# A fused transformer layer: the second MLP projection through its rank-64 factors, its residual added on GpSimd, deeper input buffers

## The reference

```python
h = hidden_states + attn_out
x2 = _layernorm(h, ln2_g, ln2_b)
hmid = jax.nn.gelu(x2 @ fc1_U @ fc1_V + fc1_b, approximate=True)   # 512 wide
mlp_out = hmid @ fc2_U @ fc2_V + fc2_b     # fc2_U: 512 x 64, fc2_V: 64 x 128
return h + mlp_out
# outside: x + (that) + experts(xn)
```

## Time and profile before

| What | Value |
|---|---|
| median of 3 runs | 1167.45 us (1165.19 to 1182.71) |
| profiled execution, its own time | 1171.44 us |
| its span | 1169.7 us |
| mean granted TensorE clock | 0.91 |
| TensorE matmul busy | 1035.9 us (89%) |
| VectorE busy | 721.8 us (62%) |
| ScalarE busy | 562.6 us (48%) |
| GpSimd busy | 387.7 us (33%) |

### The profile page before, as it was taken

How to read it: one execution, slowest core, us unless ns; L and a number is a source line. 1 busy time by engine, 2 the same in 40 slices (tenths; PEclk the granted TensorE clock), 3 DMA queues, 4 the chain that set the end, 5 groups by cost and what they waited for, 6 DMA issues and landing times. The chain is left out here.

```text
span 1169.7 us, 29046 instructions
## 1 busy us (share of the span) xinstructions
PE 1035.9 (89%) x7812; PEld 813.7 (70%) x7813; DVE 721.8 (62%) x3239; ACT 562.6 (48%) x1285; POOL 387.7 (33%) x509
## 2 busy tenths in 40 slices
PE   0697388999999999999999996999999999949997
PEld 0596165665656656566666664999999999948987
DVE  6255575776767677567577783445444444446887
ACT  0372134555546545355355565555555555525442
POOL 1003633333334324233234431444444444430110
PEclk9655668999989999799799998999999999979999
DMA  7569533443434434344243411122121122144774
GB/s 223 172 217 358 119 72 73 105 117 92 112 82 100 108 96 107 63 100 107 73 112 83 102 56 44 56 64 58 55 67 57 56 58 61 49 150 128 227 226 149
DMA packets 146698, 127.35 MB, mean 109 GB/s; under 512 B 18560, under 2 KB 128512, under 8 KB 146624
## 3 DMA queue, kind: packets, MB, share of 16 engines
q1 hardware_dynamic: 117344, 72.45, 22.7%
q0 software_dynamic: 17808, 47.35, 15.2%
q10 hardware_dynamic: 11472, 6.75, 2.2%
HBM read 57.68 MB, written 43.13 MB: 86 GB/s over the span
## 5 line engine op out<-in xcount | busy, mean ns | idle before, releaser
L1201 DVE CUSTOM_DVE_ANT_0 att_masked_st<-att_m_ps,att_mask_st 128x128 bf16<-128x128 f32 (+1 forms) x1024 | 312.8, 354 | 142.0 <-PE att_m_ps L916 63.5
L1106 ACT ACTIVATE att_probs<-att_t_ps 128x512 f32<-128x512 f32 x384 | 228.0, 597 | 228.2 <-PE att_t_ps L940 217.2
L834 POOL DMA_INDIRECT slot_x<-att_xs,att_slot_now x128 | 128.0, 1000 | 307.3 <-PE att_t_ps L940 285.5
L1377 POOL DMA_INDIRECT y_scratch<-moe_y,moe_row_now x136 | 131.0, 963 | 171.4 <-DVE moe_y L1519 113.5
L1513 DVE TENSOR_TENSOR moe_hidden<-moe_gate,moe_up_ps 128x352 f32<-128x352 f32 x136 | 70.8, 521 | 122.9 <-issue 67.9
L940 PE MATMUL att_t_ps<-att_mask_ts,att_ident_b 128*128 128x256 bf16 (+1 forms) x384 | 127.5, 332 | 0.0
L1436 PE MATMUL moe_y_ps<-w_down,moe_hidden_t 128*128 (+1 forms) x816 | 113.7, 275 | 1.8 <-issue 1.2
L1473 ACT ACTIVATE moe_gate<-moe_gate_ps 128x352 f32<-128x352 f32 x136 | 63.1, 464 | 100.3 <-PE moe_up_ps L1419 100.3
L1436 PEld LDWEIGHTS moe_y_ps<-w_down,moe_hidden_t 128*128 128x128 f32 (+1 forms) x816 | 101.7, 191 | 2.5 <-issue 2.4
L939 PE MATMUL att_t_ps<-att_odd_stack,att_k_stack 97*128 97x512 f32 x192 | 86.7, 452 | 1.9 <-DMA att_odd_stack<-att_neg_max 1.6
L955 PE MATMUL att_pv_ps<-att_probs,att_v_ones 128*32 128x256 f32 x1024 | 86.5, 411 | 0.0
(11 more groups left out here) (248 smaller groups left out, 2151.3 us busy)
## 6 DMA issues: line engine op xcount, KB each, us to landing
slot_x<-prep_blank POOLq DMA_DIRECT2D x17, 516.0 KB, 12.7
moe_x<-slot_x SPq DMA_DIRECT2D x34, 258.0 KB, 3.0
att_xs<-xn_scratch SPq DMA_DIRECT2D x32, 256.0 KB
att_k_stack<-att_k_hi POOLq DMA_DIRECT2D x64, 128.0 KB
mlp_rows<-y_scratch POOLq DMA_DIRECT2D x16, 512.0 KB, 4.8
xn_scratch<-prep_xn SPq DMA_DIRECT2D x16, 256.0 KB, 2.4
xt_scratch<-prep_xt SPq DMA_DIRECT2D x16, 256.0 KB, 2.1
att_xt<-xt_scratch SPq DMA_DIRECT2D x16, 256.0 KB, 2.6
```

Source lines behind the costliest of these rows:

```text
L834: pool.indirect_dma_start(env["slot_x"][:], bass.IndirectOffsetOnAxis(ap=slot_now[c.parity][:, col:col + 1], axis=0), xs[c.parity][:, t, k ...
L1106: act.activation(probs[:, m % PT, :], t_ps[m % 2][:], ACT.Exp).then_inc(exp_done, 1)
L1201: last = dve.tensor_tensor_reduce(out=masked_st[m % 2][:, part], in0=m_ps[m % 2][:, part], in1=mask_st[:, SEQ - width:], scale=1.0, scalar ...
L1377: pool.indirect_dma_start(env["y_dram"][:], bass.IndirectOffsetOnAxis(ap=row_now[q.parity][:, t:t + 1], axis=0), y[c.parity][:], None).the ...
```

## The change

1. `prepare` no longer forms `w2`. The two factors are loaded as they are: `fc2_left` (512 x 64 as 4 pieces of 128 x 64) and `fc2_right`, which holds `fc2_V` twice, in partitions 0 to 63 and 64 to 127 (one more DMA). Eight TensorE instructions and two ScalarE copies go.
2. fc2 of a chunk becomes `fc2_rank` (four fp32 matmuls with a 128 x 64 piece of `fc2_left` as weights and 512 columns of `mid` moving; pieces 0 and 2 add up in partitions 0 to 63 of the bank `r_ps`, pieces 1 and 3 in partitions 64 to 127), a copy of `r_ps` to SBUF by ScalarE, and `fc2_out` one step later (four fp32 matmuls, 128 x 128 weights from the copy, 128 columns of `fc2_right`) into a single bank `o_ps`. The contraction over 128 partitions in `fc2_out` adds the two halves.
3. x + h + bias is formed in place in the x buffer by two POOL instructions a chunk (`add_ahead`), behind POOL's load of the expert rows of the same chunk. VectorE keeps L1775 and L1780, one step later than before. At the start POOL issues its four loads ahead of `w1_lo`.
4. h is read once. h and x have four buffers; h of the first four chunks is loaded without a wait, later ones six chunks ahead of the store.

```diff
-                def fc2(c, t):
-                    if t == 0:
-                        pe.wait_ge(mid_ready, HCH * (c.index + 1))
-                        if not (isinstance(c.index, int) and c.index < 2):
-                            pe.wait_ge(total_ready, c.index - 1)
-                    for k in range(HCH):
-                        last = pe.matmul(o_ps[c.parity][:, t * P:(t + 1) * P], mid[c.parity][:, k, t * P:(t + 1) * P], w2[:, k, :],
-                                         start=(k == 0), stop=(k == HCH - 1))
+                def fc2_rank(c, pair):
+                    pe.wait_ge(mid_ready, HCH * c.index + 2 * pair + 2)
+                    if pair == 0 and not (isinstance(c.index, int) and c.index == 0):
+                        pe.wait_ge(rank_ready, c.index)
+                    for j in range(2):
+                        last = pe.matmul(r_ps[j * RANK_MLP:(j + 1) * RANK_MLP, :], fc2_left[:, 2 * pair + j, :], mid[c.parity][:, 2 * pair + j, :],
+                                         start=(pair == 0), stop=(pair == 1), skip_group_check=True)
+                    if pair == 1:
+                        last.then_inc(rank_done, 1)
+                def fc2_out(c):
+                    pe.wait_ge(rank_ready, c.index + 1)
+                    if not (isinstance(c.index, int) and c.index == 0):
+                        pe.wait_ge(fc2_taken, c.index)
+                    for t in range(TPC):
+                        last = pe.matmul(o_ps[:, t * P:(t + 1) * P], rank[:, t * P:(t + 1) * P], fc2_right[:], start=True, stop=True)
+                    last.then_inc(fc2_done, 1)
...
-                    for k in range(HCH):
-                        if left > 1:
-                            fc1(at(half, d + 1), k)
-                        fc2(at(half, d), k)
+                    if left > 1:
+                        fc1(at(half, d + 1), 0)
+                    if not first:
+                        fc2_out(at(half, d - 1))
+                    if left > 1:
+                        fc1(at(half, d + 1), 1)
+                    fc2_rank(c, 0)
+                    if left > 1:
+                        fc1(at(half, d + 1), 2)
+                        fc1(at(half, d + 1), 3)
+                    fc2_rank(c, 1)
...
+                def copy_rank(c):
+                    act.wait_ge(rank_done, c.index + 1)
+                    if not (isinstance(c.index, int) and c.index == 0):
+                        act.wait_ge(fc2_done, c.index)
+                    act.copy(rank[:], r_ps[:]).then_inc(rank_ready, 1)
...
+                def add_ahead(quad, k):
+                    index = AHEAD * quad + k
+                    pool.wait_ge(h_loaded[k], 16 * (quad + 1))
+                    pool.wait_ge(x_loaded[k], 16 * (quad + 1))
+                    pool.tensor_tensor(x[k][:], x[k][:], h[k][:], ALU.add).then_inc(h_added, 1)
+                    pool.wait_ge(h_added, index + 1)
+                    pool.tensor_tensor(x[k][:], x[k][:], fc2_bias[:].unsqueeze(1).to_broadcast([P, TPC, P]), ALU.add).then_inc(x_ready, 1)
...
-                    dve.tensor_tensor(sums[:], x[c.parity][:], h_again[c.parity][:], ALU.add).then_inc(sum_step, 1)
-                    dve.tensor_tensor(sums[:], sums[:], fc2_bias[:].unsqueeze(1).to_broadcast([P, TPC, P]), ALU.add).then_inc(sum_step, 1)
-                    dve.tensor_tensor(sums[:], o_ps[c.parity][:].rearrange("p (t d) -> p t d", d=P), sums[:], ALU.add).then_inc(sum_step, 1)
+                    dve.tensor_tensor(sums[:], o_ps[:].rearrange("p (t d) -> p t d", d=P), x[k][:], ALU.add).then_inc(fc2_taken, 1)
...
-                    add_up(quad, d)
+                    add_up(quad, d - 1)
```

More of the change, by code:

```diff
@@ L323, in _ @@
                 load(fc1_v[:], w["fc1_V"])
-                load(fc2_u[:], w["fc2_U"].rearrange("(c p) r -> p c r", p=P))
-                load(fc2_v[:], w["fc2_V"])
+                load(fc2_left[:], w["fc2_U"].rearrange("(c p) r -> p c r", p=P))
+                for k in range(2):
+                    load(fc2_right[k * RANK_MLP:(k + 1) * RANK_MLP, :], w["fc2_V"])
                 act.dma_start(w_router[:], w["Wr"]).then_inc(router_loaded, 16)
@@ L1556, in mlp_and_combine @@
         mid = s.two("mid", [P, HCH, CHUNK])
-        h = s.two("h", [P, TPC, P])
-        x = s.two("x", [P, TPC, P])
-        h_again = s.two("h_again", [P, TPC, P])
+        rank = s.sb("rank", [P, CHUNK])
         total = s.two("total", [P, TPC, P])
         AHEAD = 4
+        h = [s.sb(f"h{k}", [P, TPC, P]) for k in range(AHEAD)]
+        x = [s.sb(f"x{k}", [P, TPC, P]) for k in range(AHEAD)]
         rows = [s.sb(f"rows{k}", [P, 2 * TPC, P]) for k in range(AHEAD)]
         t_ps = [s.ps(f"t_ps{k}", [P, CHUNK]) for k in range(2)]
+        r_ps, o_ps = s.ps("r_ps", [P, CHUNK]), s.ps("o_ps", [P, CHUNK])
         f_ps = [s.ps(f"f_ps{k}", [P, CHUNK]) for k in range(HCH)]
-        o_ps = [s.ps(f"o_ps{k}", [P, CHUNK]) for k in range(2)]
         ln_step = s.sem("ln_step")
@@ new lines, in load_x @@
+                def load_x(index):
+                    k = index % AHEAD
+                    if index >= AHEAD:
+                        sp.wait_ge(fc2_taken, index - (AHEAD - 1))
+                    sp.dma_start(x[k][:], env["x_tiles"][:, ds(index * TPC, TPC), :]).then_inc(x_loaded[k], 16)
+                for k in range(AHEAD):
+                    load_h(k)
+                    load_x(k)
+                for k in range(2):
+                    load_h(AHEAD + k)
+                for c in range(chunks):
+                    if c + AHEAD < chunks:
+                        load_x(c + AHEAD)
+                    sp.wait_ge(total_ready, c + 1)
+                    sp.dma_start(env["out_tiles"][:, ds(c * TPC, TPC), :], total[c % 2][:]).then_inc(stored[c % 2], 16)
+                    if c + AHEAD + 2 < chunks:
+                        load_h(c + AHEAD + 2)
@@ L1671, in step @@
+                def fc2_out(c):
[5 more added lines that the diff above has]
+                    last.then_inc(fc2_done, 1)
                 def step(half, d, left):
+                    c = at(half, d)
+                    first = isinstance(c.index, int) and c.index == 0
@@ L1690, in _ @@
                 step(chunks // 2 - 1, 1, 1)
+                fc2_out(at(chunks // 2 - 1, 1))
             @block.scalar
@@ L1718, in _ @@
                     gelu(at(0, 0), k, True)
-                step(0, 0, 3, True)
+                step(0, 0, 3)
                 step(0, 1, 3)
@@ L1724, in _ @@
                 step(chunks // 2 - 1, 0, 2)
+                step(chunks // 2 - 1, 1, 1)
+                copy_rank(at(chunks // 2 - 1, 1))
             @block.vector
```

150 lines of the change are left out of this document (61 added, 89 removed).

## The result

The changed kernel takes 1180.58 us (median of 20 runs), the kernel before, run beside it, 1170.74 us (median of 20 runs). The ratio is 1.0071 with a 95% interval of 1.0042 to 1.01: slower by 0.7%, where a gain of 0.95% was forecast, and above the forecast's own range of 1153 to 1161 us as well as the wider one of 1150 to 1171. The profiled execution has a span of 1175.6 us, 5.9 above the profiled one before; 1158.6 had been predicted.

A forecast was written before the change was run, and what follows sets the result against it. Took TensorE and VectorE both as full in the last stage. TensorE's step falls from 6.89 to 6.26 us; with start, tail and fold, 11.1 us less: 1167.45 - 11 = 1156.5 us, own range 1153 to 1161.

The forecast's parts named there:

- the wider one: Whole-kernel range of 1150 to 1171 us, taking in rival 3, most of rival 2 and the three-round form.
- What POOL's adds cost: Last stage: POOL's two adds, 2.6 us a chunk, hold only VectorE's weighted sums, by 0 to 1.3 us, 0.6 taken.
- signs of being wrong: Last stage: rank records evenly spaced at 0.43 us, VectorE's step over 7 us, or TensorE waiting for `copy_rank`.
- The second rival: Last stage: POOL's adds hold VectorE fully, 2.6 us, VectorE's step 8.2 us, total 1171 us; chance 0.15.
- The start: Start of the last stage: 1.0 us charged for POOL holds, bounds 0 to 2.6; fc1 of chunk 1 at 1055.8.
- are not waited for at once: Start of the last stage: extra h, x and expert-row loads issued ahead make nothing wait at once.
- rival 1: Last stage, `fc2_rank`: pairs do not run together, 3.46 instead of 1.73 us, total 1184 us; chance 0.13 with three-round form.
- three-round form: Last stage, `fc2_rank`: records start in program order, +0.43 us twice a chunk, 1170 us; chance 0.13 with rival 1.
- Rival 3: TensorE in the last stage: mode changes cost nothing where other waits cover them, 6.7 us less, 1150 us; chance 0.10.
- The fold's 0.35 us: Fold in `prepare`: dropping four transposes saves about 0.86 us, one more DMA costs about 0.5; net -0.35 us.
- B: Experiments' theory, last stage: TensorE's new chain (rank matmuls, copy, `fc2_out`) has its own wait that sets the 8.0 us step.
- C: Experiments' theory, last stage: the deeper loads come late or delay others; step near 8.0 us.

The follow-up runs named there:

- e7: Kernel before, with two idle POOL adds on buffers of their own behind the loads of the last 12 chunks; one run, 1193.85 us.
- e1: Changed kernel with the two adds a chunk moved from POOL to VectorE; ratio to before 0.9913 (0.9833 to 0.9993).
- e9: Changed kernel with SP loading h of chunks 0 to 3 before x, and POOL making `w1_lo` before its four loads; one run, 1173.8 us.
- e6: Changed kernel with adds on VectorE, normalise on ScalarE and a chunk's rank matmuls all in one row; one run, 1153.29 us.
- e2: Changed kernel with one POOL add a chunk instead of two, leaving out the fc2 bias; ratio to before 1.0053 (0.9994 to 1.0113).
- e3b: Changed kernel with POOL's adds of a chunk waiting for the next chunk's normalise; one run, 1168.74 us; the same kernel timed again, ratio 1.0001.
- e5: Changed kernel with the normalise moved to ScalarE as four activations, the adds staying on POOL; one run, 1181.92 us.

## Why the prediction was wrong

**The step that failed** is "What POOL's adds cost". It found that POOL can hold VectorE, with the 0.91 us of the earlier trace rows, and then took only the instructions that read two SBUF tensors for holdable. The normalise reads one tensor and two columns of scalars; I counted it, by name, among the cover under which the first add would lie free. e7 shows the reverse: it is held for the whole length of each add. So the hold was 2.7 us a chunk in place of 0 to 1.3 (0.6 taken), VectorE's step 8.17 us on average in place of 5.54 to 6.84, and the 14 steps 103.8 us in place of 86.3. These 17.5 us, 2.5 of the start and 0.9 of the tail, less the 4.2 by which the stages ahead were shorter (0.3 of it forecast, for the fold), are the 17 us between the forecast span and the measured one. Of the prediction's signs of being wrong, a VectorE step over 7 us is the one that came.

The second rival had the mechanism ("or a normalise that is held too") and the step, 8.2 us. Its 1171 us are still 10 below the measured time: the kernel before, run again beside it, was 3.3 us above the median that the forecast started from, and the rest is the steps (17.5 us, not 15), the start and the tail. Its 0.15 was too small: what spoke against it was the timing of the adds, which was right (they begin 1.5 us behind the sum, as computed) and pointed at the normalise itself. The trace of before had a sign that I did not look for. Its normalise has a median of 0.342 us and a longest of 0.582 us; in e1, where POOL likewise only issues loads, such a record (0.59 us) ends with POOL's issue. The single records' longest, not the mean, would have asked the question.

Two sections of the Trainium skill, put together, foretold it. Page "VectorE: DVE Perf Modes", section "The perf-mode tier table (the rule you actually need)", places a `tensor_scalar` of fp32 data in SBUF in the mode that uses both read ports. Page "SBUF — State Buffer", section "SBUF: two separate sides", which I had cited, puts such instructions under the exclusive lock beside those with two SBUF inputs. The trace agrees that such an instruction is blocked and not slowed: it takes 2.0 us beside an add in place of 0.34. The same page gives the lock to whichever instruction starts first; by the records, the third normalise starts 0.6 us ahead of the add (during POOL's DMA issue) and is blocked all the same. The first page cites 2x for the speed, which no run here shows: four normalises take 1.11 us, and eight weighted sums, with two tensors read, 2.42, so 0.28 against 0.30 us for the same 128 columns.

**The start** was charged 1.0 us and bounded by 2.6. Chunk 1 came at 18.7 us, 2.5 later than forecast. What failed is the sentence that the extra loads ahead "are not waited for at once": h of chunk 1, now issued behind x of chunk 0, landed 11.7 us after the stage's start, and fc1 of chunk 0 waited for it; with h ahead of x (e9) chunk 1 came at 15.0 us. The holds by POOL's DMA issues were not counted either, but lay under that wait.

**What held.** The rank matmuls run in pairs: four records in 1.08 us for two rounds, and e6's eight in 1.87 from start to start. The first part of rival 1 and its three-round form are out. TensorE's own step was 6.48 us against 6.26: `fc2_out` 0.89 as predicted, the rank matmuls and changes of mode (6.48 - 0.44 - 2.78 - 0.89) = 2.37 against 2.15, chiefly as one change costs 0.36 and not 0.21 us. Rival 3 is out too. The copy (0.585 us) is hidden in the loop; TensorE waits for it only in the last two chunks, 1.4 us in all. VectorE's step without the hold is 8.0 - 2.74 = 5.26 us against 5.37, and e2 gives the same (6.92 - 1.66). With the hold away, e3b's 14 steps take 89.4 us against the 86.3 forecast. The fold's 0.35 us can't be read: the first matmul of attention starts at 128.5 us before and 126.0 after, but at 126.4 in e7, which has before's fold.

B and C fell with e1, e3b and e7. In e5 the loads are those of after, and its step is TensorE's own.

## What to carry to other kernels

An elementwise instruction moved to GpSimd is free only if VectorE runs nothing meanwhile that GpSimd holds up, and in this kernel that was the one-tensor fp32 normalise from SBUF to SBUF as much as the two-tensor sums, and not the instructions that read PSUM. So list what each engine's order puts beside the moved work: an add that is released by the event that also releases VectorE's next instruction meets the same one in every step, and one more wait can place one of two adds beside PSUM reads instead (8.0 to 6.45 us, with 1.1 us of hold left from the other). A held instruction counts as busy in the profile: look for an engine whose busy share rose while its instruction count fell. Loads issued ahead of need can delay the one that is needed first; keep that one in front.

## What the hardware showed that I had not expected

- The normalise beside a GpSimd add takes up to 2.0 us instead of 0.34, and one that begins during the DMA issue ahead of the add is held to the add's end (1.66 us for an add of 1.30).
- GpSimd's DMA issues alone hold VectorE as well: L149 took 1.45 us in place of 0.20 and ended with the last issue. In e9 two `tensor_scalar` instructions took 0.42 and 0.53 us and ended with the first and the second issue, while the two-input instructions beside the same issues kept their 0.23 us.
- Changing from fp32r work of full width to 64-column fp32 tiles and back costs 0.36 us, and a pair of fp32 matmuls to the two column halves takes the time of one (0.43 to 0.48 us for each of its two rounds).
